# A decoder layer with attention replaced by an LRU, a Toeplitz mixer and routed experts: the norm of the next group, the query products and the Toeplitz tables are arranged anew

## The chip, the cores and the metric

One NeuronCore of a Trainium2 chip runs the whole kernel in one launch. The metric is device time in microseconds (us); the times given are medians over executions. The engines are PE (TensorE, matmuls), DVE (VectorE), ACT (ScalarE), POOL (GpSimd) and SP (SyncE, which here only issues DMAs).

## The reference, cut to what matters

`x` is 16 sequences of 128 tokens with 256 features. Everything is fp32.

```python
# block 1: gated linear recurrence and an MLP
xn = rmsnorm(x, norm1_w)
left  = gelu(xn @ left_W + left_b)
right = rg_lru(causal_depthwise_conv(xn @ right_W + right_b, conv_w, conv_b), ...)   # two gates, a scan over time
x1 = left * right @ out_W + out_b + x
x1n = rmsnorm(x1, norm2_w)
x = layernorm(x + gelu(x1n @ up1_W) * (x1n @ up2_W) @ down_W + down_b + x1)          # biases of up left out here
# block 2: 16 heads of width 8 over the 128 tokens; the features (256) are the time axis of the convolution
kv  = einsum('bhil,bhjl->bijhl', ctx, ctx)            # symmetric in i, j: 36 pairs per head
out = causal_conv(kv, ssm_kernel) + kv * D            # a 256-tap Toeplitz product per head
x = layernorm(x + einsum('bijhl,bhil->bjhl', out, x))
# block 3: 64 experts, top 6, capacity 64 over the first tokens that vote for an expert, and a shared expert
x = layernorm(x + moe(x))
```

## The kernel before, in words

The 16 sequences are worked in G = 4 groups of NB = 4 sequences (512 tokens). `over_groups` (L265) calls `step(gh, gt, gs)` on every engine: the head (block 1) of group gh, the tail (block 2, the norm and the router of block 3) of group gh-1, and the shared expert of group gh-2, in one step. There are five steps: step 0 has a head only, step 1 head and tail, steps 2 and 3 (the body of a hardware loop, L269) all three, and the last one tail and shared expert. Then come the voting rounds and shared expert of the last group, 32 pairs of routed experts, and the final sums and norm. Each engine has its own instruction stream, written out in order by hand; semaphores tie them together, and an engine that waits holds everything behind it.

**Start.** SP issues (L293 to L316) x of group 0, four constants, five weight matrices on one semaphore (`weights_in`), then `krep_dram`, a copy of the padded taps with 128 rows per head in DRAM, the context, the shared weights, and behind a wait the read of the Toeplitz tables `toep` from `krep_dram` with a stride one shorter than a row (L308). Then it zeroes the accumulation buffer `y_dram` (L314 to L316, 6.6 MB) and loads x and context of the further groups (L317). PE's first dense product waits for all five weights (L747). POOL adds D to the diagonal of the 16 tables (L385, L388) before it forms the residual sums `xo = x + out_b` (L407) and `xs = x + down_b` (L413), and the pair products of the context (L397).

**Head.** ACT squares and sums x (`mean_square`, L518), takes the root (L529); DVE scales x to `xn` (`norm_apply`, L1015); PE transposes it into `tb` (L671); DVE copies it to `xT` (`feature_copy`, L1020); PE forms right and left (`dense`, L677); ACT evacuates (L542, L546); DVE does the 4-tap convolution (L1095, L1101); PE forms two gates; ACT evacuates (L553) and takes tanh and exp (L559, L561) and root (L568); DVE multiplies (L1117 to L1130), scans (L1132) and multiplies by left (L1135, `lr_s`); PE forms the output product (L803); DVE adds (L1143); a second norm (L518, L578, L1146, L1015, L671, L1020); six times two up products (L829, recorded at L677), gelu on ACT (L588) and product on DVE (L1168); then four blocks of down products (L840), and residual and statistics on DVE (L1206, L1210).

**Tail.** PE multiplies the Toeplitz tables into the pair products (`conv`, L723 to L725, heads 0 to 7 at the start of the step, 8 to 11 behind the dense products, 12 to 15 behind the gates), ACT evacuates to `ycv` (L513). DVE normalises block 1's output to `x2` (L1072), PE transposes, DVE copies to `q` (L1107). `query_products` (L964) multiplies q into ycv and sums over i: for each distance d of the pair (i, j) two products into `tmp` (L975) and two sums into `acc` (L980), 29 instructions for a group of heads. DVE has 11 heads, in slices of five instructions between its L1168 (L1170), POOL has 5. PE transposes `acc` (L859), then norm, router product (L877), softmax, top 6 and votes on DVE.

**Shared.** `votes_by_expert` (L709) puts the votes of group gs by expert; DVE picks the first 64 tokens of each in 8 `rounds` of max and replace (L1037, L1039), four before its 4-tap convolution and four after the copy to q (L1087, L1109). The shared expert is L696 and L705 on PE, L506 on ACT, L1050 and L1055 on DVE.

**Waits.** In the loop a wait's value is computed in a register (`wait_apart`, L256). `keep_clock` (L680) issues matmuls of zeros where PE has nothing to do: 8 at the start, 7 in step 0 and 5 in step 1 behind the gates, 6 in the last step.

## Time and profile before

| | |
|---|---|
| median of 3 executions | 668.96 us |
| lowest, highest | 667.96, 676.25 us |
| profiled execution: time, span | 671.55 us, 669.9 us |
| mean granted TensorE clock, as a share of 2.4 GHz | 0.892 |
| busy: PE, DVE, POOL, ACT | 522.3, 373.4, 277.8, 212.7 us |
| down products end (step 0, 1, 2, 3) | 110.9, 202.8, 307.0, 411.2 us |
| experts begin | 499.6 us |

The rows below come from one profiled execution. A row gives the start in us, the time from the start to the end of the group, the engine, the line, what is written and read, and in brackets the idle time of the engine before it and what ended it. A matmul in fp32 leaves two records. A PE record of 512 columns takes 0.43 us at 2.4 GHz and 0.85 us at 1.2 GHz.

### The profile page before, as it was taken

To read this page: it belongs to the slowest core of one execution; us is meant where nothing else is said; L and a number is where in the kernel's file an instruction comes from. 1 tells how busy PE (TensorE), PEld (TensorE's weight loads), DVE (VectorE), ACT (ScalarE), POOL (GpSimd) and SP (SyncE) were. 2 spreads that over 40 slices of the span, in tenths; PEclk is the share of its full clock that TensorE was granted. 3 is DMA by queue.
4 is the path that set the end of the run, shared out by engine and by line. 5 is a ranking of instruction groups with operands and counts; after the bars stand their busy time and mean duration, and the time that the engine had idled before them with its cause. 6 is when DMAs were issued, how large, how long until landed. Compare 5 with 4: busy or idle time off the path is not lost.

```text
span 669.9 us, 7127 instructions
## 1 busy us (share of the span) xinstructions
PE 522.3 (78%) x2181; PEld 313.8 (47%) x2181; DVE 373.4 (56%) x850; ACT 212.7 (32%) x431; POOL 277.8 (41%) x340
## 2 busy tenths in 40 slices
PE   5863699975986987996887998948779887779075
PEld 2322349543466543566543468615345433334065
DVE  2357224553968983967985766995753212123037
ACT  4350232452124472315472314311203221213024
POOL 1029301537505437503545701690036455457500
PEclk9795699986998988999998999968979988889579
DMA  8996100100001101001200000886229999975596
GB/s 300 173 362 264 33 0 1 32 1 31 0 1 39 32 1 31 1 32 40 96 0 0 0 31 35 265 238 186 97 55 274 314 300 290 303 239 66 55 380 247
DMA packets 30702, 81.17 MB, mean 121 GB/s; under 512 B 3248, under 2 KB 16048, under 8 KB 30544
## 3 DMA queue, kind: packets, MB, share of 16 engines
q1 hardware_dynamic: 23328, 66.48, 30.9%
q0 software_dynamic: 7344, 14.32, 9.3%
q8 instruction: 15, 0.25, 0.1%
q14 instruction: 15, 0.12, 0.1%
HBM read 62.80 MB, written 21.13 MB: 125 GB/s over the span
## 4 chain that ended last, share of the span: by engine, by line
PE 49%; DVE 27%; issue 11%; DMA 5%; ACT 5%; SPq 1%; DVEq 0%; ACTq 0%; POOLq 0%
PE mb L677 15%; PE kb L840 6%; PE mb L920 5%; PE kb L939 4%; PE kb L705 4%; DMA y_dram<-cregion,y_all 3%; DVE first L1037 3%; DVE cand L1039 3%; PE kb L803 3%; DVE hregion L1015 2%; DVE cregion L980 2%; DMA wregion<-in_w_down_dram 2%; DVE cregion L975 2%; PE mb L960 2%; PE tb L960 1%
## 5 line engine op out<-in xcount | busy, mean ns | idle before, releaser
L677 PE MATMUL mb<-hregion,wregion 128*128 128x512 f32 x320 | 155.3, 645 | 16.6 <-DVE hregion L1020 5.4
L677 PEld LDWEIGHTS mb<-hregion,wregion 128*128 128x128 f32 x320 | 65.3, 208 | 99.5 <-issue 85.7
L397 POOL TENSOR_TENSOR cregion<-ctxT 128x256 f32<-128x256 f32 (+7 forms) x128 | 68.4, 568 | 77.9 <-PE mb L725 77.9
L463 POOL DMA_INDIRECT y_dram<-cregion,y_all x32 | 50.3, 1573 | 44.3 <-DVE cregion L1309 40.2
L1309 DVE TENSOR_SCALAR cregion<-kb,prob 128x256 f32<-128x256 f32 x32 | 15.5, 484 | 77.5 <-issue 67.2
L840 PE MATMUL kb<-wregion,hregion 128*128 128x256 f32 x192 | 43.7, 382 | 5.2 <-DVE hregion L1168 5.2
L588 ACT ACTIVATE hregion<-mb,cols 128x512 f32<-128x512 f32 x24 | 16.5, 687 | 92.5 <-PE mb L677 92.5
L454 POOL DMA_INDIRECT hregion<-rows_dram,idx_all x32 | 31.3, 978 | 32.1 <-DVE idx_all L1283 19.0
L1168 DVE SCALAR_TENSOR_TENSOR hregion<-mb,cols,hregion 128x512 f32<-128x512 f32 x24 | 17.9, 746 | 43.9 <-PE mb L677 43.9
L840 PEld LDWEIGHTS kb<-wregion,hregion 128*128 128x128 f32 x192 | 35.7, 190 | 13.0 <-DVE hregion L1168 4.6
L980 POOL TENSOR_TENSOR cregion<-cregion 128x280 f32<-128x280 f32 (+6 forms) x56 | 40.6, 725 | 2.2
L975 POOL TENSOR_TENSOR cregion<-cregion 128x280 f32<-128x280 f32 (+6 forms) x56 | 37.7, 673 | 4.4
L437 POOL DMA_DIRECT2D rows_dram<-rows x4 | 3.1, 770 | 82.6 <-DVE rows L1244 82.6
L696 PE MATMUL mb<-x3T,wsh 128*128 128x512 f32 x64 | 30.3, 626 | 5.0 <-ACT cregion L513 4.0
L683 PE MATMUL mb<-zeros,ident 128*128 128x512 f32 x52 | 28.7, 712 | 6.0 <-ACT cregion L513 2.9
L975 DVE TENSOR_TENSOR cregion<-cregion 128x616 f32<-128x616 f32 (+6 forms) x56 | 31.6, 565 | 1.6
L980 DVE TENSOR_TENSOR cregion<-cregion 128x616 f32<-128x616 f32 (+6 forms) x56 | 31.7, 567 | 0.7
L803 PE MATMUL kb<-wregion,hregion 128*128 128x256 f32 x64 | 17.7, 438 | 18.4 <-DVE hregion L1135 18.4
L671 PE MATMUL tb<-ident,hregion 128*128 128x128 f32 x64 | 12.0, 350 | 22.9 <-DVE hregion L1015 22.9
L513 ACT ACTIVATE cregion<-mb 128x288 f32<-128x288 f32 x64 | 23.8, 408 | 17.3 <-PE mb L725 17.3
L705 PE MATMUL kb<-wshd,shh 128*128 128x256 f32 (+1 forms) x96 | 26.8, 442 | 3.2 <-DVE shh L1050 3.2
L615 ACT ACTIVATE wregion<-mb 88x256 f32<-88x256 f32 x32 | 12.2, 380 | 51.9 <-PE mb L929 51.9
(186 smaller groups left out, 1000.3 us busy)
## 6 DMA issues: line engine op xcount, KB each, us to landing
hregion<-in_w_experts_dram SPq DMA_DIRECT2D x12, 704.0 KB
wregion<-in_w_experts_dram SPq DMA_DIRECT2D x11, 704.0 KB
y_dram<-zeros SPq DMA_DIRECT2D x4, 1536.0 KB, 14.4
hregion<-in_w_experts_down_dram SPq DMA_DIRECT2D x12, 352.0 KB
cregion<-in_w_experts_dram SPq DMA_DIRECT2D x6, 704.0 KB
wregion<-y_dram SPq DMA_DIRECT2D x8, 512.0 KB, 6.6
hregion<-y_dram SPq DMA_DIRECT2D x8, 512.0 KB, 14.0
wregion<-in_w_experts_down_dram SPq DMA_DIRECT2D x11, 352.0 KB
```

Of the source, the lines that this page charges most:

```text
L397: last = e.tensor_tensor(v.kv[:, hb % 2, :, :, DOFF[d] * NB:DOFF[d] * NB + n], cx[:, :, :, 0:n], cx[:, :, :, d * NB:d * NB + n], ALU.mult)
L454: e.indirect_dma_start(out=v.xg[:, r, :], out_offset=None, in_=v.rows_dram[:, :], in_offset=bass.IndirectOffsetOnAxis(ap=v.idx_all[:, p:p ...
L463: e.indirect_dma_start(out=v.y_dram[:, :], out_offset=bass.IndirectOffsetOnAxis(ap=v.y_all[:, p:p + 1], axis=0), in_=v.dout[:, r, :], in_o ...
L677: last = e.matmul(bank, w[:, c, n0:n0 + P], rhs[:, c, :], start=(c == 0), stop=(c == C - 1))
L683: e.matmul(bank[:], v.ident[:], v.zeros[:, 0:512], start=True, stop=True)
L696: last = e.matmul(banks[k][0:n, :], v.wsh[:, c, k * FS + f * P:k * FS + f * P + n], v.x3T[:, c, :], start=(c == 0), stop=(c == C - 1))
L705: last = e.matmul(kb[k][:, b * D:(b + 1) * D], v.shh[0:n, f, t0:t0 + S], v.wshd[0:n, f, :], start=(f == 0), stop=(f == NF - 1))
L803: last = e.matmul(kb[k][:, b * D:(b + 1) * D], v.left[:, c, t0:t0 + S], v.wo[:, c, :], start=(c == 0), stop=(c == C - 1))
L840: last = e.matmul(kb[k][:, b * D:(b + 1) * D], v.mlp[:, j, t0:t0 + S], v.wdn[:, j, :], start=(j == 0), stop=(j == FJ - 1))
L920: last = e.matmul(mb[p % 2][x * CAP:(x + 1) * CAP, 0:2 * FE], v.xgT[:, p % 2, c, x * CAP:(x + 1) * CAP], wgu[:, x, c, :], start=(c == 0), ...
L975: steps.did(e.tensor_tensor(v.tmp[:, t, :, heads, 0:n], v.q[:, :, heads, cols], y, ALU.mult))
L980: steps.did(e.tensor_tensor(v.acc[:, :, heads, cols], v.acc[:, :, heads, cols], v.tmp[:, t, :, heads, 0:n], ALU.add))
```

## The change: what it does

The taps are loaded to 16 partitions, DVE adds D to tap 0, and they are written back to DRAM once. Each partition p then reads 256 taps of each head from offset p on (a Hankel table, 2 MB in rows of 1 KB), and PE multiplies by a flipped identity (8 matmuls of 512 columns, behind the gates of step 0, where `keep_clock` was), which turns it into the Toeplitz table; ACT evacuates it (8 copies). Each weight has a semaphore of its own. The norm of group g+1 is made in step g: squares and root on ACT after the gelus, scaling on DVE after the query products, transposes on PE (into `mb`) behind the first down product and the transposes of acc, the copy to xT on DVE before the first residual. The votes and all 8 rounds of group gs now stand behind the copy to q. POOL makes the products of the context first, the residual sums behind q, and waits for x1n before it adds `xo` to `xs`. The query products go by 32 pairs of feature half and head: distances d and 8-d share one full-width temporary, so that 15 instructions do what 29 did; DVE has 22 of the 32 and POOL 10, the same shares. The loops over groups are written out. `load_x(1)` stands ahead of the zeroing of `y_dram`, `load_ctx(1)` behind it.

```diff
@@ -30,7 +30,8 @@
 HEADS = S // HD
-HEADS_DVE = 11
+CH = 2 * HEADS
+CH_DVE = 22
...
@@ -185,13 +187,14 @@
         v.ctxT = sb("ctxT", [P, C, S * NB])
-        cregion = sb("cregion", [P, 10752])
+        cregion = sb("cregion", [P, 11008])
...
         v.ycv = take(C * HEADS * PW, cregion).rearrange("p (c h n) -> p c h n", c=C, h=HEADS)
+        v.hankel = v.ycv.rearrange("p c h n -> p (c h n)")[:, 0:HEADS * 2 * P].rearrange("p (h n) -> p h n", h=HEADS)
...
         v.acc = take(C * HEADS * HD * NB, cregion).rearrange("p (c h n) -> p c h n", c=C, h=HEADS)
-        v.tmp = take(2 * C * HEADS * (HD - 1) * NB, cregion).rearrange("p (t c h n) -> p t c h n", t=2, c=C, h=HEADS)
+        v.tmp = take(2 * CH * HD * NB, cregion).rearrange("p (t g n) -> p t g n", t=2, g=CH)
...
@@ -266,7 +270,7 @@
     step(1, 0, None)
-    with e.Fori(2, G) as g:
+    for g in range(2, G):
...
@@ -290,23 +294,28 @@
+        e.dma_start(v.taps, v.kpad_in).then_inc(s["taps_in"], 16)
+        e.dma_start(v.d_sb[:], v.d_in.rearrange("o h -> h o")).then_inc(s["taps_in"], 16)
         load_x(0)
...
+        e.dma_start(v.cols[:], v.cols_in).then_inc(s["consts_in"], 16)
+        e.dma_start(v.wlr, v.wlr_in).then_inc(s["w_lr"], 16)
+        e.dma_start(v.outb[:], v.outb_in.to_broadcast((P, D))).then_inc(s["consts_in"], 16)
+        e.dma_start(v.downb[:], v.downb_in.to_broadcast((P, D))).then_inc(s["consts_in"], 16)
+        e.dma_start(v.wg, v.wg_in).then_inc(s["w_gates"], 16)
+        e.dma_start(v.wo, v.wo_in).then_inc(s["w_out"], 16)
         load_ctx(0)
+        e.dma_start(v.wup, v.wup_in).then_inc(s["w_up"], 16)
+
+        e.wait_ge(s["taps_s"], 1)
+        e.dma_start(v.taps_dram, v.taps).then_inc(s["taps_out"], 16)
+        e.dma_start(v.wdn, v.wdn_in).then_inc(s["w_down"], 16)
+        e.wait_ge(s["taps_out"], 16)
+        k = v.taps_dram[0:HEADS, 0:1]
+        e.dma_start(v.hankel, bass.AP(k.tensor, k.offset, [[1, P], [KW, HEADS], [1, 2 * P]])).then_inc(s["tables"], 16)
...
+        load_x(1)
...
@@ -314,7 +323,8 @@
         e.dma_start(yv[:, NBLK, rest:], v.zeros[:, 0:D]).then_inc(s["zero_out"], 16)
-        with e.Fori(1, G) as g:
+        load_ctx(1)
+        for g in range(2, G):
...
@@ -373,19 +384,17 @@
+        e.memset(v.flip, 0.0).then_inc(s["flip_s"], 1)
+        e.wait_ge(s["flip_s"], 1)
+        e.affine_select(out=v.flip, in_=v.flip, compare_op=ALU.not_equal, fill=1.0, base=1 - P,
+                        pattern=[[E, 2], [1, E]], channel_multiplier=1).then_inc(s["flip_s"], 1)
...
+        e.wait_ge(s["consts_in"], 16 * 3)
...
@@ -399,34 +408,32 @@
         def step(gh, gt, gs):
+            if gt is not None:
+                products(gt, 2)
+                products(gt, 3)
...
-
-                if not (isinstance(gh, int) and gh == 0):
+                if gt is not None:
+
+                    wait(e, s["q_s"], 2 * gt + 2)
...
                 if gt is not None:
-                    products(gt, 2)
-                if gt is not None:
...
                     .then_inc(s["xs_s"], 1)
-            elif gt is not None:
-                products(gt, 2)
-            if gt is not None:
-                products(gt, 3)
-            if gh is not None:
...
                 wait(e, s["x1_s"], 2 * gh + 2)
+                wait(e, s["x1n_s"], 4 * gh + 4)
...
                 wait(e, s["q_s"], 2 * gt + 2)
-                for f in query_products(e, v, psteps, slice(HEADS_DVE, HEADS)):
+                for f in query_products(e, v, psteps, slice(CH_DVE, CH)):
...
@@ -505,6 +512,12 @@
+        def taps_turned(n0, banks):
+            for n, bank in enumerate(banks):
+                e.wait_ge(s["turned"], n0 + n + 1)
+                e.activation(v.toep[:, 2 * (n0 + n):2 * (n0 + n) + 2, :], bank[:].rearrange("p (h n) -> p h n", h=2), ACT.Copy)\
+                    .then_inc(s["toep_s"], 1)
...
@@ -518,17 +531,18 @@
-            if head:
-                wait(e, s["x_in"], 16 * gh + 16)
-                if not (isinstance(gh, int) and gh == 0):
-                    wait(e, s["x1_tr"], 2 * gh)
+            def norm_root(g):
+                wait(e, s["x_in"], 16 * g + 16)
+
+                wait(e, s["x1_tr"], 2 * g)
                 mean_square(v.xin, v.ss1, "ss1_s")
-                wait(e, s["ss1_s"], gh + 1)
-                if not tail:
-                    e.wait_ge(s["consts_s"], 1)
+                wait(e, s["ss1_s"], g + 1)
+                e.wait_ge(s["consts_s"], 1)
                 e.activation(v.rms1, v.ss1, ACT.Sqrt, scale=1.0 / D, bias=v.eps_rms[:]).then_inc(s["rms1_s"], 1)
-                if not tail:
-                    softplus()
+
+            if head and not tail:
+                norm_root(0)
+                softplus()
...
@@ -566,6 +580,9 @@
                     e.activation(v.th[:, c, :], v.th[:, c, :], ACT.Sqrt).then_inc(s["mult_s"], 1)
+            if not tail:
+                taps_turned(0, (kb[0], kb[1], v.tb[0], v.tb[1]))
+                taps_turned(4, mb)
...
@@ -587,6 +604,8 @@
                         .then_inc(s["gelu_s"], 1)
+                if gh + 1 < G:
+                    norm_root(gh + 1)
...
@@ -711,6 +730,10 @@
+        def turn_taps(n0, banks):
+            for n, bank in enumerate(banks):
+                e.matmul(bank[:], v.flip, v.hankel[:, 2 * (n0 + n):2 * (n0 + n) + 2, :], start=True, stop=True).then_inc(s["turned"], 1)
...
@@ -725,39 +748,44 @@
-            if tail:
-                e.wait_ge(s["d_done"], 2)
+            def features(g):
+                wait(e, s["xn_s"], 4 * g + 4)
+                for k in range(2):
+                    transposes(v.xn, k, "x_tr", mb)
+
+            if tail:
+                e.wait_ge(s["toep_s"], HEADS // 2)
+                if head:
+                    wait(e, s["xT_s"], 4 * gh + 4)
...
             if head:
-                wait(e, s["xn_s"], 4 * gh + 4)
-                if gs is not None:
-                    wait(e, s["x3T_s"], 2 * gt)
-                    wait(e, s["logit_read"], gt)
-                for k in range(2):
-                    transposes(v.xn, k, "x_tr")
-            if gs is not None:
-                wait_apart(e, v, s["y_s"], 2 * gt + 2)
-                wait_apart(e, v, s["dve_r"], RDVE * gt)
-                votes_by_expert(gs)
-            if head:
-                e.wait_ge(s["weights_in"], 16 * 5)
+                if not tail:
+                    features(0)
+                e.wait_ge(s["w_lr"], 16)
...
                     dense(mb[k][:], v.wlr, (k + 2) % 4 * P, v.xT, "lr_done")
+            if gs is not None and not head:
+                wait_apart(e, v, s["y_s"], 2 * gt + 2)
+                wait_apart(e, v, s["dve_r"], RDVE * gt)
+                votes_by_expert(gs)
...
                 wait(e, s["x2_s"], 4 * gt + 4)
-                if not head:
-                    wait(e, s["x3T_s"], 2 * gt)
-                    wait(e, s["logit_read"], gt)
+                wait(e, s["x3T_s"], 2 * gt)
+                wait(e, s["logit_read"], gt)
...
                     transposes(v.x2, k, "x2_tr")
+                if gs is not None and head:
+                    wait(e, s["y_s"], 2 * gt + 2)
+                    wait(e, s["dve_r"], RDVE * gt)
+                    votes_by_expert(gs)
...
@@ -787,11 +816,17 @@
                         wait(e, s["conv_evac"], HEADS * gt + HEADS)
+                        keep_clock(mb[3], 5)
                     else:
+                        e.wait_ge(s["flip_s"], 2)
+                        e.wait_ge(s["tables"], 16)
+                        turn_taps(0, (kb[0], kb[1], tb[0], tb[1]))
                         wait(e, s["gate_s"], 4 * gh + 4)
-                    keep_clock(mb[3], 5 if tail else 7)
+                        turn_taps(4, mb)
+                        e.wait_ge(s["toep_s"], 2)
                 wait(e, s["lr_s"], C * gh + C)
+                e.wait_ge(s["w_out"], 16)
...
@@ -823,7 +860,7 @@
                         elif i < 4:
-                            wait(e, s["gate_s"], 4 * gh + i + 1)
+                            wait(e, s["toep_s"], HEADS // 4 + i + 1)
...
@@ -861,6 +899,8 @@
             if head:
+                if gh + 1 < G:
+                    features(gh + 1)
...
@@ -961,29 +1001,46 @@
+def query_products(e, v, steps, part):
+
+    n_part = part.stop - part.start
+    WIDE = HD * NB
+    y = v.ycv.rearrange("p c h n -> p (c h) n")[:, part]
+    q = v.q.rearrange("p c h n -> p (c h) n")[:, part]
+    acc = v.acc.rearrange("p c h n -> p (c h) n")[:, part]
+    tmp = v.tmp[:, :, part]
+
+    def pair_of(ap, at, step, n):
+        return bass.AP(ap.tensor, ap.offset + at, [list(ap.ap[0]), [step, 2], list(ap.ap[-2]), [1, n]])
+
+    def both(d, low):
...
         n = (HD - d) * NB
...
+        lo = tmp[:, low]
+        hop = (CH * WIDE) * (1 - 2 * low)
+        yd = y[:, :, DOFF[d] * NB:DOFF[d] * NB + n]
+        wait(e, steps.sem, steps.base + steps.n)
+        steps.did(e.tensor_tensor(pair_of(lo, d * NB, hop - d * NB, n), pair_of(q, 0, d * NB, n), pair_of(yd, 0, 0, n), ALU.mult))
+
+    def diagonal():
+        steps.did(e.tensor_tensor(acc, q, y[:, :, 0:WIDE], ALU.mult))
+
+    def middle():
+        d = HD // 2
+        n = d * NB
+        yd = y[:, :, DOFF[d] * NB:DOFF[d] * NB + n]
+        wait(e, steps.sem, steps.base + steps.n)
+        steps.did(e.tensor_tensor(pair_of(tmp[:, 0], n, -n, n), pair_of(q, 0, n, n), pair_of(yd, 0, 0, n), ALU.mult))
+
+    def add(t, behind):
+        wait(e, steps.sem, steps.base + steps.n - behind)
+        steps.did(e.tensor_tensor(acc, acc, tmp[:, t], ALU.add))
+
+    parts = [diagonal]
+    for d in range(1, HD // 2):
+        parts += [lambda d=d: both(d, 1), lambda d=d: both(HD - d, 0), lambda: add(0, 0), lambda: add(1, 0)]
+    parts += [middle, lambda: add(0, 0)]
+    assert len(parts) == QSTEPS
...
@@ -1009,16 +1066,18 @@
         e.wait_ge(s["tnum_s"], 1)
+        e.wait_ge(s["taps_in"], 32)
+        e.tensor_tensor(v.taps[:, P - 1:P], v.taps[:, P - 1:P], v.d_sb[:], ALU.add).then_inc(s["taps_s"], 1)
...
-        def feature_copy(k, name, done):
+        def feature_copy(k, name, done, banks=tb):
...
                 e.tensor_scalar(v.xT[:, c, k * 2 * S:(k + 1) * 2 * S].rearrange("p (b s) -> p b s", b=2),
-                                tb[k][:].rearrange("p (b c s) -> p b c s", b=2, c=C)[:, :, c, :],
+                                banks[k][:].rearrange("p (b c s) -> p b c s", b=2, c=C)[:, :, c, :],
...
@@ -1057,12 +1116,21 @@
             head, tail = gh is not None, gt is not None
+            def norm_one(g):
+                wait(e, s["rms1_s"], g + 1)
+                e.reciprocal(v.inv1, v.rms1).then_inc(s["inv1_s"], 1)
+                wait(e, s["inv1_s"], g + 1)
+                norm_apply(v.xn, v.xin, v.inv1, "xn_s")
+
+            def features(g):
+                for k in range(2):
+                    wait(e, s["x_tr"], 2 * g + k + 1)
+                    feature_copy(k, "norm1", "xT_s", mb)
...
                 hsteps.begin(gh)
-                wait(e, s["rms1_s"], gh + 1)
-                e.reciprocal(v.inv1, v.rms1).then_inc(s["inv1_s"], 1)
-                wait(e, s["inv1_s"], gh + 1)
-                norm_apply(v.xn, v.xin, v.inv1, "xn_s")
+                if not tail:
+                    norm_one(0)
...
@@ -1073,18 +1141,15 @@
                 if not tail:
-                    e.wait_ge(s["consts_in"], 16 * 4)
-                for k in range(2):
-                    wait(e, s["x_tr"], 2 * gh + k + 1)
-                    feature_copy(k, "norm1", "xT_s")
-                if not tail:
+                    e.wait_ge(s["consts_in"], 16 * 3)
+                    features(0)
...
                     e.tensor_scalar(v.lru[:, 0], v.lru[:, 0], LRU_C, None, ALU.mult).then_inc(s["lru_s"], 1)
-            if gs is not None:
+            if gs is not None and not head:
...
@@ -1107,6 +1172,9 @@
             if gs is not None:
+                if head:
+                    votes_in(gs)
+                    rounds(0, 4)
...
@@ -1167,15 +1235,17 @@
                                            in1=v.gl[:, j % 2, :], op0=ALU.add, op1=ALU.mult).then_inc(s["h_s"], 1)
-                    for f in parts[5 * j:5 * j + 5]:
+                    for f in parts[QPART * j:QPART * j + QPART]:
...
                 for n, f in enumerate(parts):
-                    if gs is not None and n in (4, 8, 12):
-                        shared_rows(gs, n // 4 - 1)
-                    if gs is not None and n == 24:
+                    if gs is not None and n in (2, 4, 6):
+                        shared_rows(gs, n // 2 - 1)
+                    if gs is not None and n == 12:
...
                     f()
+            if head and gh + 1 < G:
+                norm_one(gh + 1)
...
@@ -1211,6 +1281,8 @@
             if head:
+                if gh + 1 < G:
+                    features(gh + 1)
```

## Rows read from the trace of the kernel before

**Rows 1.** The page: busy time by engine, its share of the span, instructions.

```profile
PE 522.3 (78%) x2181; PEld 313.8 (47%) x2181; DVE 373.4 (56%) x850; ACT 212.7 (32%) x431; POOL 277.8 (41%) x340
```

**Rows 2.** Timeline of step 0, all engines, 8 to 69 us.

```profile
8.14 1.14 DVE L1015 TENSOR_SCALAR hregion<-hregion,st 128x256 f32<-128x256 f32 x4
...
17.69 9.96 PE L677 MATMUL mb<-hregion,wregion 128*128 128x512 f32 x16 [5.37 <-DMA wregion<-in_w_down_dram]
...
45.07 0.68 DVE L1130 TENSOR_TENSOR hregion<-hregion 128x512 f32<-128x512 f32 x1
...
45.84 4.57 POOL L385 TENSOR_TENSOR cregion<-ident,d_sb 128x2048 f32<-128x2048 f32 x1 [42.46 <-DMA wregion<-krep_dram]
...
47.04 3.91 DVE L1135 TENSOR_TENSOR hregion<-hregion 128x512 f32<-128x512 f32 x1
...
61.87 6.62 PE L803 MATMUL kb<-wregion,hregion 128*128 128x256 f32 x16 [16.44 <-DVE hregion L1135]
```

**Rows 3.** Timeline of DVE in step 1: the same instruction, and the last of the sequence, 144 to 150 us.

```profile
144.59 0.69 DVE L1130 TENSOR_TENSOR hregion<-hregion 128x512 f32<-128x512 f32 x1 [0.17 <-ACT hregion L568]
...
149.16 0.69 DVE L1135 TENSOR_TENSOR hregion<-hregion 128x512 f32<-128x512 f32 x1
```

**Rows 4.** DMA issues, from the page of DMAs: KB each, us to landing.

```profile
krep_dram<-in_kpad_dram SPq DMA_DIRECT2D x1, 3064.0 KB, 29.8
...
wregion<-krep_dram SPq DMA_DIRECT2D x1, 2048.0 KB, 9.8
```

**Rows 5.** Timeline of PE: the dense products that open the head of steps 1, 2 and 3; behind the gates of step 3.

```profile
119.04 7.11 PE L677 MATMUL mb<-hregion,wregion 128*128 128x512 f32 x16 [1.36 <-issue]
...
216.88 7.65 PE L677 MATMUL mb<-hregion,wregion 128*128 128x512 f32 x16 [0.33 <-DVE hregion L1020]
...
320.48 7.13 PE L677 MATMUL mb<-hregion,wregion 128*128 128x512 f32 x16 [0.35 <-DVE hregion L1020]
...
353.16 3.72 PE L803 MATMUL kb<-wregion,hregion 128*128 128x256 f32 x16 [1.01 <-DVE hregion L1135]
```

**Rows 6.** Timeline of DVE in step 3, and a round of the last step.

```profile
341.91 1.23 DVE L1117 TENSOR_TENSOR hregion<-hregion 128x1024 f32<-128x1024 f32 x1
...
359.92 2.94 DVE L1015 TENSOR_SCALAR hregion<-hregion,st 128x256 f32<-128x256 f32 x4
...
420.60 0.75 DVE L1037 MAX8 first<-cand 64x8 f32<-64x576 f32 x1
...
422.23 0.75 DVE L1037 MAX8 first<-cand 64x8 f32<-64x576 f32 x1
```

**Rows 7.** Groups by shape: query products, and a copy of a PSUM bank on ACT.

```profile
L975 DVE TENSOR_TENSOR cregion<-cregion 128x616 f32<-128x616 f32 x8 | 7.9, 984 | 0.3
...
L598 ACT ACTIVATE x3T<-tb 128x512 f32<-128x512 f32 x8 | 4.3, 594 | 10.5 <-PE tb L671 10.5
...
L975 DVE TENSOR_TENSOR cregion<-cregion 128x264 f32<-128x264 f32 x8 | 3.5, 433 | 0.3
...
L975 DVE TENSOR_TENSOR cregion<-cregion 128x88 f32<-128x88 f32 x8 | 2.0, 246 | 0.2
```

**Rows 8.** Timeline of POOL in step 1: query products with DVE idle.

```profile
157.81 1.63 POOL L975 TENSOR_TENSOR cregion<-cregion 128x280 f32<-128x280 f32 x2
...
164.11 1.29 POOL L975 TENSOR_TENSOR cregion<-cregion 128x200 f32<-128x200 f32 x2
```

**Rows 9.** Timeline of PE and DVE: down products of step 1, and the last step.

```profile
187.59 2.86 PE L840 MATMUL kb<-wregion,hregion 128*128 128x256 f32 x12 [2.04 <-DVE hregion L1168]
...
461.20 1.29 DVE L1186 TENSOR_TENSOR u<-tb,x 128x512 f32<-128x512 f32 x2 [2.43 <-DMA y_dram<-u]
```

**Rows 10.** Windows: us, PE, PEld, DVE, ACT, POOL busy, granted clock, DMA share, GB/s.

```profile
7.00:12.00 5.00, 5.00 (x18) 2.56 (x17) 1.33 (x6) 4.14 (x8) 0.00 (x0) 1.00 1.02 410
...
18.00:24.00 6.00, 6.00 (x8) 2.38 (x8) 0.55 (x1) 0.69 (x1) 0.00 (x0) 0.55 1.08 177
...
62.00:70.00 8.00, 6.49 (x16) 4.90 (x16) 1.38 (x2) 0.74 (x4) 7.15 (x17) 0.64 0.00 1
```

63 lines of the change are left out of this document (17 added, 46 removed).

## The prediction

> **What bounds the kernel now.** I read the page first, then the chain that ended last, then the timeline of each engine by step, and the groups by shape for prices. PE is busy for 78% of the span, DVE for 56% [rows 1], and in the chain PE has half the time and DVE a quarter. So PE is the resource, and time is to be had only where PE waits. These places differ by step. In step 0 PE waits 5.37 us for the last of five weights although it needs the first, and 16.44 us for DVE's scan and product [rows 2]. That second wait is not DVE work: L1135 takes 3.91 us there [rows 2] and 0.69 us in step 1 [rows 3], because POOL's table sums (4.57 us, and one more of that size behind) run at the same time. At the head of steps 1, 2 and 3 PE stands still for the norm of x (dense products at 119.04, 216.88 and 320.48, while the step before ended at 110.9, 202.8 and 307.0) [rows 5]. The reader should see in each row's bracket who was late.
>
> **Start, step 0.** x's DMA goes out two issues later, about 1 us. The dense product now needs its own weights alone, so up to 5.4 us are free [rows 2]. But POOL's two residual sums (L407 and L413, 1024 elements each; POOL takes 2.1 ns an element and 0.25 us, so 2.4 us [rows 8]) no longer stand behind the tables; they become ready when the constants land, at about 9 us, just when DVE scales x (4 instructions, 1.14 us alone, 8.14) [rows 2]. In step 3, DVE's same four instructions took 2.94 us beside one such POOL sum [rows 6]. Beside two they would take up to 5 us, end near 15 instead of 9.3, and the dense product would start at 17.4 instead of 17.69: gain 0.3. If DVE is first, it starts at 13.9, and PE, with a pause of 1.5 instead of 5.4 us, may keep 2.4 GHz (7 to 12 us) instead of falling to 1.2 GHz (clock 0.55, 18 to 24 us) [rows 10], which is worth some 3 us more: gain 6.8. I take 1.5, near the lower end, since POOL's start and DVE's are within a microsecond of each other.
>
> **The tables.** The DRAM copy of 3064 KB (29.8 us to landing) goes, and the read stays as large (2048 KB, 9.8 us) [rows 4]. It is issued when the 24 KB of taps have landed behind some 4 MB of earlier loads; at 300 GB/s (an estimate from the 410 and 177 GB/s of the windows [rows 10]) this is at 16 us, and the table lands at 26 to 29, ahead of the end of the gates at 37. POOL's two sums leave DVE's way. From L1130 to the output product step 1 takes 144.59 to 149.9, 5.3 us [rows 3]; step 0 took 45.07 to 61.87, 16.8 us [rows 2]. Gain 11.5. The new work is 8 matmuls, 16 records of 0.43 us, 6.9 us in the place of `keep_clock`, and 8 ACT copies of 0.594 us [rows 7], 4.8 us behind ACT's roots. Both lie beside the 5.3 us of DVE; PE needs only two of the copies before its output product, the other six before the up products 7 us on. I cost them at nothing. Without this cover they would cost up to 5 us. Moving `load_x(1)` ahead of the zeroing costs nothing: x of group 1 is wanted after the gelus, 20 us later. The zeroing (6.6 MB, 15 us of issue) and `load_ctx(1)` behind it have until step 1. Separate semaphores for the later weights wait for nothing: all have landed by 20 us.
>
> **The norm made ahead.** The transposes (8 records, 1.0 us of PE) move from the head of steps 1 to 3 into steps 0 to 2: plus 1.1 us in each of these (3.3 in all), and minus their share at the head. ACT's squares, table and root take 3.6 us behind the last gelu, then DVE 1.3; PE in this time has its first down block (2.9 us [rows 9]) and, with a tail, the transposes of acc, so xn is late by at most 0.3 us. DVE's copies (1.7 us) stand before a residual that has 2.7 us of idle time behind it. With x ready, the dense products start when the 8 heads of convolution end, 5.95 us into the step (24 triples at 0.245). Before, they started 8.1, 14.0 and 13.5 us in [rows 5]. Gross gain 2.2, 8.1 and 7.5.
>
> **The rounds behind q.** In steps 2 and 3 this is partly given back, because DVE fills the gap with nothing. Step 3 counted from the dense products: right lands at 2.4 and 4.2 us, the 4-tap convolution ends at 8.7, copy to q at 10.7, votes at 11.5, eight rounds at 24.6 (pitch 1.64 us, 420.60 to 422.23 [rows 6]), so L1117 starts at 24.9. (An estimate: landing times, the convolution's 4.5 us, q's 2.0 and the rounds are taken as step 3 shows them.) Before, it started at 341.91 - 320.48 = 21.4 [rows 5, 6]. The gates then are no longer last, DVE is. Behind L1117 the way to the output product is 7.9 to 8.9 us, and before it waited a little for ACT's exp, so 1.3 (step 2) to 2.0 us (step 3) are given back at the output product. The net gain there is 6.8 and 5.5.
>
> **POOL behind x1n.** DVE's second scaling no longer meets the sum L424: 2.94 us become 1.14 [rows 6, 2], in steps 1, 2 and 3: 1.8 each. POOL's queue: the products of group gt come first, and PE wants the first at 12 us into the step; the query products start 2.3 us later, and have over 20 us until PE transposes acc.
>
> **Query products.** Elements stay the same (22 x 480 = 10560 on DVE). An instruction of 88 elements takes 246 ns and one of 264 takes 433 [rows 7], so 1.06 ns an element and 0.15 us each; with POOL at work 616 take 984 [rows 7], 1.4 ns an element. 14 instructions fewer are 2.1 us less on DVE in each of four passes. Only what DVE is late for counts: in step 1 the down products wait 2.04 us for L1168 [rows 9], I take 1.8; in steps 2 and 3 shared work covers it, 0; in the last step DVE is the chain, but the shared expert's product and the storing DMA stand between (2.43 us of its wait [rows 9]): I take 3.0 in all.
>
> **Clock.** PE's pause before the output product of steps 2 and 3 grows from 1.0 [rows 5] to about 4 us. After a long pause the same 16 records took 6.62 us [rows 2] at clock 0.64 [rows 10], against 3.72 [rows 5]. Cost 0 to 2.9 twice, I take 1.0 each.
>
> **The sum.** Step 0: 1.5 + 11.5 - 1.1 = 11.9. Step 1: 2.2 + 1.8 + 1.8 - 1.1 = 4.7. Step 2: 6.8 + 1.8 - 1.1 = 7.5. Step 3: 5.5 + 1.8 = 7.3. Last 3.0. Clock -2.0. Together 32.4. The experts and final sums (from 499.6 us on) keep their length. The profiled execution took 671.55 us, 2.6 over the median, so 639.2 for it and 668.96 - 32.4 = 636.6 for the median; I say 636.5.
>
> **Weighed against the Trainium skill.** A rule that speaks against wide instructions is in "SBUF — State Buffer", section "Who interferes with whom": DVE with two SBUF inputs and POOL lock each other out for a whole instruction. Step 0 agrees (3.91 us for 0.69 [rows 2, 3]). By it, fewer and longer POOL instructions hold DVE longer each time; as a mechanism of this kernel it is the second rival. "Runtime: NRT & Kernel Launch", section "Instruction fetch mechanics", says that a taken branch can force a fetch of code; the trace shows no gap on PE at the loop's turn (the last product ends at 307.0, and the table products follow at once), so by the trace unrolling gives nothing, and by the page it would give one fetch, which no row here prices.
>
> **Rivals.** *First: x is scaled before POOL's sums, and the clock stays up.* Start gain 6.8 instead of 1.5, clock loss 0: 636.5 - 7.3 = 629. For it: DVE's scaling begins at about 9.2 and takes 1.1. Against: the constants land at the same time. 0.2. *Second: the port.* The POOL query products (up to 560 elements, about 1.4 us) and DVE's run one after the other in all four passes: DVE's 13.4 us (10560 x 1.06 ns and 15 x 0.15 us [rows 7]) wait for 5 to 6 of POOL's 13.8 (4800 x 2.1 ns and 15 x 0.25 us [rows 8]), beyond the slack of 2 us: 4 x 3.5 = 14, so 650. For it: 984 ns where 803 are due [rows 7]. Against: POOL starts 9 us before DVE and has few left. 0.12. *Third: the table is late.* A hot 24 KB in DRAM, read 85 times over, at half the speed (20 us): it lands at 37 to 40, where PE wants it at 37; the turning then ends up to 3 us behind the scan and ACT's copies delay x1; with a low clock 8 us: 644. 0.13. *Fourth, the other side: the paired products are slow.* Their access patterns step over two halves with runs of 4 to 28 elements; were they to cost more per element on DVE, 4928 elements in each of four passes would be late. The gain of 32.4 is gone when each pass is 8.1 + 3 of slack late, 2.3 ns an element more (three times today's price); at 3.0 ns more it is 4 x (14.8 - 3) = 47 late, 684, slower by over 2%. Against: today's form has as many dimensions and runs of 4 to 28 too, at 246 ns for 88 elements [rows 7]. 0.03.
>
> **How the numbers follow.** Forecast 0.52. The range takes in the first rival and the start's full gain (down to 624), and the second and third (up to 650). Two per cent, 13.4 us, is about what a measurement of this kernel can tell from no change. Faster than 655.6: all but part of the rivals' upper ends, 0.94; within 2% 0.04; slower 0.02.
>
> **What would show it.** Right: the output product of step 0 at about 49 us with no long DVE instruction before; dense products 6 us after each step's first convolution, with no idle time; L1117 ending the gates' wait in steps 2 and 3; the second scaling at 1.1 us. Wrong: a PE wait on the DMA of the Hankel table; PE waiting for xn behind the first down block; query products beyond 1.5 us on DVE; a clock of 0.55 through the up products.

## The result, and the profile after

The changed kernel took 649.07 us (median of 4 executions, 646.63 to 655.09). Beside it the kernel before took 672.55 us, and the ratio is 0.967 (95% interval 0.956 to 0.977): faster by 3.3% where 4.8% were forecast. 649.07 lies at the upper edge of the range, 624 to 650. A second series gave a ratio of 0.960 (0.950 to 0.970). All ratios leave out executions over 1.5% above the fastest of the same kernel, and of the traces shown only e1's is of such a slower execution.

To see where the time went I cut each trace where DVE ends the last residual sum of a step (L1206 before, L1276 after), and at PE's first expert product. The two traces of the changed kernel agree within 0.1 us on each of these marks.

| us | step 0 | step 1 | step 2 | step 3 | last step | experts begin | rest of the span |
|---|---|---|---|---|---|---|---|
| before | 111.7 | 91.9 | 104.1 | 104.2 | 87.7 | 499.6 | 170.3 |
| changed | 93.9 | 91.5 | 99.7 | 98.4 | 86.9 | 470.4 | 173.8 |
| changed, second trace | 93.9 | 91.5 | 99.7 | 98.4 | 86.9 | 470.5 | 170.7 |
| gain | 17.8 | 0.4 | 4.4 | 5.8 | 0.8 | 29.2 | |
| forecast | 11.9 | 4.7 | 6.5 | 6.3 | 3.0 | 32.4 | 0 |

(The forecast's 2.0 us for the clock are taken off steps 2 and 3 here.) The sum up to the experts is nearly right, and the steps are not: step 0 gave 6 us more, the others gave 9 us less. So the near hit is in part luck. Step 0 also varies from trace to trace: in the ten traces of kernels that differ in nothing that step 0 executes it took 91.3 to 96.2 us. Busy time on the page answers to [rows 1]; PE has as much work as before in less time:

```profile
PE 520.1 (81%) x2183; PEld 316.0 (49%) x2183; DVE 368.1 (57%) x795; ACT 217.0 (34%) x439; POOL 251.9 (39%) x284
```

**Step 0** answers to [rows 2]. Timeline of the changed kernel, DVE, POOL and PE:

```profile
8.75 1.14 DVE L1074 TENSOR_SCALAR hregion<-hregion,st 128x256 f32<-128x256 f32 x4
...
10.48 2.34 POOL L420 TENSOR_TENSOR hregion<-hregion,outb 128x1024 f32<-128x1024 f32 x1 [6.70 <-DMA downb<-in_down_b_dram]
...
14.27 7.11 PE L696 MATMUL mb<-hregion,wregion 128*128 128x512 f32 x16 [1.48 <-DVE hregion L1079]
24.88 8.61 PE L696 MATMUL mb<-hregion,wregion 128*128 128x512 f32 x16 [3.51 <-DVE hregion L1166]
...
40.19 0.68 DVE L1198 TENSOR_TENSOR hregion<-hregion 128x512 f32<-128x512 f32 x1
...
44.75 0.69 DVE L1203 TENSOR_TENSOR hregion<-hregion 128x512 f32<-128x512 f32 x1
...
45.54 5.09 PE L838 MATMUL kb<-wregion,hregion 128*128 128x256 f32 x16 [5.18 <-ACT wregion L518]
```

The reader sees DVE scale x before POOL's sums begin, the dense products at 14.27 at full clock (16 records in 7.11 us), and the scan with no stretched instruction: L1203 takes 0.69 us where L1135 took 3.91. From the first product behind the roots to the output product are 5.35 us, as forecast. (The last bracket names an ACT copy. By the code PE wants only the first two of the eight, which had ended by 41.9; the last it waits for is L1203, which ends at 45.44.)

**Step 1.** Timeline of PE in the changed kernel:

```profile
98.86 7.03 PE L696 MATMUL mb<-hregion,wregion 128*128 128x512 f32 x16
...
129.65 3.72 PE L838 MATMUL kb<-wregion,hregion 128*128 128x256 f32 x16 [0.98 <-DVE hregion L1203]
...
166.88 4.54 PE L877 MATMUL kb<-wregion,hregion 128*128 128x256 f32 x12 [3.78 <-DVE hregion L1236]
```

The dense products start without a wait 5.8 us after the down products of step 0, where they took 8.1 before. DVE's first slice of the MLP is 4.7 us earlier in the step (at 52.2, before 56.9). Then it is lost: from the first to the last h DVE takes 20.0 us where it took 18.3, the first down block waits 3.78 us for the last h (2.04 before [rows 9]), and it takes 4.54 us instead of 2.86, most of it at half the clock.

**Step 3.** Timeline of the changed kernel, DVE at the head, then PE behind the gates:

```profile
289.31 2.76 DVE L1324 TENSOR_TENSOR votes<-mask,tnum 128x256 f32<-128x256 f32 x1
292.10 0.73 DVE L1327 TENSOR_SCALAR tnum<-tnum 128x4 f32<-128x4 f32 x1
...
292.94 3.61 DVE L1140 TENSOR_SCALAR x<-hregion,mv,st 128x256 f32<-128x256 f32 x4
...
317.06 1.23 DVE L1185 TENSOR_TENSOR hregion<-hregion 128x1024 f32<-128x1024 f32 x1
```

```profile
326.18 6.42 PE L838 MATMUL kb<-wregion,hregion 128*128 128x256 f32 x16 [3.79 <-DVE hregion L1203]
...
339.27 14.00 PE L696 MATMUL mb<-hregion,wregion 128*128 128x512 f32 x32 [1.31 <-DVE hregion L1079]
...
367.54 2.86 PE L877 MATMUL kb<-wregion,hregion 128*128 128x256 f32 x12 [1.99 <-DVE hregion L1236]
```

L1324 takes 2.76 us where the same product took 0.43 at 312.01 before, and the four x2 scalings 3.61 for 1.46: POOL's products of the table, moved to the head, run at 289.2 to 296.3. DVE's gate product comes 27.0 us after the first dense product instead of the forecast 24.9; PE then pauses 3.8 us, and its output product takes 6.42 us instead of 3.72 [rows 5]. Two things stand against this. DVE's head was not free of POOL before either: beside a POOL sum and eight products L1255 took 2.23 us, where the same instruction takes 0.17 in e1, and the scaling of x took 2.27 for 1.14. And PE gets clock back further on. Its first 32 records of up products take 14.00 us, and took 17.02 before (15.69 in step 2):

```profile
365.46 17.02 PE L677 MATMUL mb<-hregion,wregion 128*128 128x512 f32 x32 [1.39 <-DVE hregion L1020]
```

So my theory for the experiments was: from step 1 on DVE is last, not PE; it loses time beside POOL, PE's pauses grow, and PE's clock falls behind them. Rivals: the query products' new form is itself slower or saves nothing; the norm made ahead was never the limit; the last part of the kernel got longer by the change.

### The profile page after: what moved, and what is told of

Read it like the earlier page. It is cut to its first block, busy times and chain, and to the rows that moved or that the text cites. A ratio compares the mean times of both kernels' runs of the same rounds, so it can differ in the third digit from the quotient of the medians.

```text
span 644.2 us, 6592 instructions
## 1 busy us (share of the span) xinstructions
PE 520.1 (81%) x2183; PEld 316.0 (49%) x2183; DVE 368.1 (57%) x795; ACT 217.0 (34%) x439; POOL 251.9 (39%) x284
## 4 chain that ended last, share of the span: by engine, by line
PE 50%; DVE 31%; issue 10%; DMA 4%; ACT 3%; POOL 0%; POOLq 0%; DVEq 0%; SPq 0%
PE mb L696 14%; PE kb L877 7%; PE mb L960 5%; PE kb L979 4%; DVE cand L1098 4%; DMA y_dram<-cregion,y_all 4%; DVE first L1096 4%; PE kb L838 3%; PE mb L702 2%; PE kb L724 2%; DVE cregion L1037 2%; DVE hregion L1166 2%; DVE x L1140 2%; PE kb L715 2%; PE mb L1000 2%
## 5 line engine op out<-in xcount | busy, mean ns | idle before, releaser
L696 PE MATMUL mb<-hregion,wregion 128*128 128x512 f32 x320 | 145.8, 613 | 9.9 <-DVE hregion L1079 6.0
L696 PEld LDWEIGHTS mb<-hregion,wregion 128*128 128x128 f32 x320 | 62.0, 197 | 85.8 <-issue 73.3
L406 POOL TENSOR_TENSOR cregion<-ctxT 128x256 f32<-128x256 f32 (+7 forms) x128 | 63.1, 527 | 40.2 <-PE mb L748 40.2
L877 PE MATMUL kb<-wregion,hregion 128*128 128x256 f32 x192 | 45.5, 393 | 8.7 <-DVE hregion L1236 8.7
L431 POOL TENSOR_TENSOR hregion<-hregion 128x1024 f32<-128x1024 f32 x4 | 9.4, 2346 | 85.3 <-issue 85.3
L1236 DVE SCALAR_TENSOR_TENSOR hregion<-mb,cols,hregion 128x512 f32<-128x512 f32 x24 | 17.9, 745 | 35.2 <-PE mb L696 35.2
L838 PE MATMUL kb<-wregion,hregion 128*128 128x256 f32 x64 | 22.0, 518 | 15.4 <-DVE hregion L1203 10.3
L1037 POOL TENSOR_TENSOR cregion<-cregion 128x320 f32<-128x320 f32 x28 | 31.8, 1135 | 2.2
L1037 DVE TENSOR_TENSOR cregion<-cregion 128x704 f32<-128x704 f32 x28 | 31.2, 1113 | 0.7
L634 ACT ACTIVATE wregion<-mb 88x256 f32<-88x256 f32 x32 | 12.2, 380 | 54.1 <-PE mb L969 45.4
L1023 POOL TENSOR_TENSOR cregion<-cregion 128x560 f32<-128x560 f32 (+5 forms) x24 | 29.7, 1236 | 1.9
L1374 DVE TENSOR_TENSOR wregion<-mb,wregion 128x176 f32<-128x176 f32 x32 | 10.8, 337 | 32.5 <-ACT wregion L648 29.4
L1023 DVE TENSOR_TENSOR cregion<-cregion 128x1232 f32<-128x1232 f32 (+5 forms) x24 | 28.9, 1205 | 0.6
## 6 DMA issues: line engine op xcount, KB each, us to landing
hregion<-y_dram SPq DMA_DIRECT2D x8, 512.0 KB, 12.9
```

The lines of the kernel that those rows point to most:

```text
L406: last = e.tensor_tensor(v.kv[:, hb % 2, :, :, DOFF[d] * NB:DOFF[d] * NB + n], cx[:, :, :, 0:n], cx[:, :, :, d * NB:d * NB + n], ALU.mult)
L696: last = e.matmul(bank, w[:, c, n0:n0 + P], rhs[:, c, :], start=(c == 0), stop=(c == C - 1))
L838: last = e.matmul(kb[k][:, b * D:(b + 1) * D], v.left[:, c, t0:t0 + S], v.wo[:, c, :], start=(c == 0), stop=(c == C - 1))
L877: last = e.matmul(kb[k][:, b * D:(b + 1) * D], v.mlp[:, j, t0:t0 + S], v.wdn[:, j, :], start=(j == 0), stop=(j == FJ - 1))
L1023: steps.did(e.tensor_tensor(pair_of(lo, d * NB, hop - d * NB, n), pair_of(q, 0, d * NB, n), pair_of(yd, 0, 0, n), ALU.mult))
L1037: steps.did(e.tensor_tensor(acc, acc, tmp[:, t], ALU.add))
```

## The experiments

All steps by the marks of the table above; ratios are to the kernel before on the same chip.

**e1: POOL behind x2,** in POOL's `step`.

> The changed kernel, but POOL waits for x2 before the table products of the group being finished (one wait, nothing else). Port theory (DVE's scaling and votes are stretched because POOL's products moved beside them): the votes product falls from 2.76 us to under 1.3, the four x2 scalings from 3.6 us to under 2.0, in every step head from step 2 on; the first gate-side product of DVE then starts at most 25 us after the first dense product in step 3 (27.0 before), and steps 2 and 3 are each 1.5 to 3 us shorter: in all 3 to 6 us below the changed kernel. Rival (the contention only moves: POOL's products then stretch the 4-tap convolution and the copy to q by as much): the same DVE time between the end of the step before and the gates, no change within 1 us. A second rival: PE waits for the later tables at head 8, and the step grows.

```diff
             if gt is not None:
+                wait(e, s["x2_s"], 4 * gt + 4)
                 products(gt, 2)
```

Ratio 0.953 (0.943 to 0.963); steps 1 to 3: 93.2, 98.5, 97.9; last step 84.0. Timeline of DVE in e1, step 3:

```profile
291.04 0.43 DVE L1325 TENSOR_TENSOR votes<-mask,tnum 128x256 f32<-128x256 f32 x1
...
291.79 1.38 DVE L1141 TENSOR_SCALAR x<-hregion,mv,st 128x256 f32<-128x256 f32 x4
294.47 0.76 DVE L1161 TENSOR_SCALAR hregion<-hregion,cols 128x512 f32<-128x512 f32 x1 [1.30 <-ACT hregion L557]
...
296.65 5.41 DVE L1167 SCALAR_TENSOR_TENSOR hregion<-hregion,cols 128x512 f32<-128x512 f32 x6
```

The stretching is gone, 5.1 us of it, so its cause is shown. But the gate product is only 1.1 us earlier in the step: DVE now waits 2.3 us for ACT's copies of the dense products, and the 4-tap convolution takes 5.41 us beside POOL instead of 4.06. In step 3 the first down block also took 4.54 us instead of 2.86, so 1.7 us of what the wait gave there went with the clock. Both theory and rival were half right. Only the last step, where DVE has no convolution, kept most of it (2.9 us); e8, e9 and e14, which have the same wait, took 83.4 to 84.5 us there.

**e2 and e15: the last parts behind the last h.** The same kernel twice, on two chips.

> The changed kernel with the 15 parts of DVE's query products cut 3, 3, 3, 2, 2, 2 over the six slices of the MLP instead of 3, 3, 3, 3, 3, 0. Theory (in step 1 the first down block waits 3.78 us and runs at the lower clock because all parts stand ahead of the last h): that wait falls to under 1.8 us in step 1, and the first down block takes 2.9 instead of 4.5 us; step 1 is 2.5 to 4 us shorter; steps 2 and 3, where shared work covers it, gain 0 to 1.5. Rival (the time is only moved to the transposes of acc, which want the last part): the step keeps its length within 0.7 us.

```diff
+QCUT = (0, 3, 6, 9, 11, 13, 15)
...
-                    for f in parts[QPART * j:QPART * j + QPART]:
+                    for f in parts[QCUT[j]:QCUT[j + 1]]:
```

> The kernel with the cut alone once more. Its steps repeat: 88.0, 97.3 and 94.8 us for steps 1 to 3. If its last part, 179.7 us in its first trace, belongs to the kernel, it is 178 to 182 again; if it belongs to the run or the chip, it comes out with that of the other kernels, 170 to 176.

e2: ratio 0.951 (0.943 to 0.959), steps 91.3, 88.0, 97.3, 94.8. e15: ratio 0.949 (0.945 to 0.954), steps 96.2, 89.9, 97.4, 96.3. So where the parts are cut is worth 1.6 to 3.6 us in each of steps 1 to 3, and the transposes of acc don't give it back. The steps did not repeat as I had expected of e15: step 1 is 1.9 and step 3 is 1.5 us longer than in e2. In step 1 the down block starts after 1.78 (e2) or 1.06 us (e15) and takes 2.86. The two traces differ in what no edit made: 4.9 us in step 0 and 1.9 in step 1. Windows of 7.2 us, from 28.5 us into step 1, e2 and then e15 (columns as in [rows 10]):

```profile
119.80:127.00 7.20, 6.26 (x10) 2.41 (x10) 6.85 (x10) 2.56 (x5) 4.00 (x5) 0.76 0.01 2
```

```profile
124.70:131.90 7.20, 4.56 (x10) 1.82 (x10) 6.86 (x10) 2.56 (x5) 4.00 (x5) 1.00 0.01 2
```

PE had done the same ahead of this. In e2 the clock falls under the five filler products (6.26 us) and is back for the output product (3.72). In e15 the fillers run at full clock in 4.56 us, the pause behind them is 2.7 instead of 1.0 us, and the output product takes 5.41. In step 0, likewise, the 16 gate records behind a pause of 3.2 to 3.5 us took 7.13 us in e2, 8.61 in the changed kernel and 10.19 in e15. The last part took 176.1 us in e15 and 179.7 in e2, so at least 3.6 us of its spread are not the kernel's.

**e3: fillers ahead of the output product of steps 2 and 3.**

> The changed kernel with four filler products (ident by zeros, 3.4 us of PE) ahead of the wait for the scan in steps 2 and 3, into the bank that the output product overwrites. Clock theory (after PE's pause of 3.8 us the output product runs at 1.2 GHz, 6.4 us for 16 records, and the transposes and part of the up products behind it too): the output product takes 3.7 us in steps 2 and 3, and each of these steps is 2.5 to 3.5 us shorter; in all 5 to 7 us. Rival (DVE is last anyway: its x1 sum and the norm only start earlier by part of it): 1 us a step or less. Steps 0 and 1 unchanged.

```diff
+                if gs is not None:
+                    wait(e, s["voteT_s"], gs + 1)
+                    keep_clock(kb[1], 4)
                 wait(e, s["lr_s"], C * gh + C)
```

Ratio 0.964 (0.958 to 0.970); steps 2 and 3: 96.7 and 97.4. The output product takes 3.72 us in both. Step 2 gained 3.0 us, step 3 only 1.0, since there the first down block then took 4.54 us instead of 2.86: the clock fell at a later pause.

```profile
323.35 3.72 PE L841 MATMUL kb<-wregion,hregion 128*128 128x256 f32 x16 [0.35 <-DVE hregion L1206]
...
361.99 4.54 PE L880 MATMUL kb<-wregion,hregion 128*128 128x256 f32 x12 [1.99 <-DVE hregion L1239]
```

**e4: four rounds into DVE's waits.**

> The changed kernel with the last four of the eight rounds of MAX8 and MATCH_REPLACE8 of steps 2 and 3 moved from ahead of DVE's gate product to its waits behind the scan (behind the shared rows, between and behind the two x1 sums, behind the second scaling). Theory (DVE's rounds are last before the gates' product and make PE pause): the gate product starts 5.5 to 6.6 us earlier, or where the gates end (about 21.4 us after the first dense product, as before the change); PE's pause before the output product goes to 1 us or less and its 16 records take 3.7 us; what the moved rounds then cost behind it is 1.6 us at most for those ahead of the second scaling. Steps 2 and 3 shorter by 4 to 7 us each, 8 to 14 us in all. Rival (the rounds are late for what follows as they were for what stood ahead): gain under 2 us a step.

```diff
-                rounds(4, 8)
-                keep_first()
...
                 shared_rows(gs, 1)
+                rounds(4, 5)
...
+                    if gs is not None and k == 0:
+                        rounds(5, 6)
+                if gs is not None:
+                    rounds(6, 7)
...
                 norm_apply(v.xn, v.xo, v.inv2, "x1n_s")
+                if gs is not None:
+                    rounds(7, 8)
+                    keep_first()
```

Ratio 0.967 (0.961 to 0.973); steps 2 and 3: 98.9 and 96.2. The gate product came 6.7 us earlier in the step (25.3 for 32.0), and the step gained 0.8 and 2.2. PE in e4, step 3:

```profile
321.56 3.72 PE L838 MATMUL kb<-wregion,hregion 128*128 128x256 f32 x16 [1.62 <-DVE hregion L1204]
326.98 3.67 PE L715 MATMUL kb<-x3T,wsh 128*96 128x512 f32 x8 [1.70 <-DVE hregion L1213]
...
334.53 2.11 PE L696 MATMUL mb<-hregion,wregion 128*128 128x512 f32 x3 [2.99 <-DVE hregion L1079]
```

The rival nearly won: rounds ahead of an x1 sum and of the feature copies are late for these (waits of 1.70 and 2.99 us). The clock took another part: the first 32 records of up products took 15.70 us in both steps for 14.00 in the changed kernel, and in step 2 the first down block took 4.29 for 2.86. DVE's only wait long enough, 5.6 us, is behind the copies.

**e5: the norm at the head again.** `norm_root`, `norm_one` and `features` at the head of each step, as before the change.

> The changed kernel with the norm of x made where it was before the change: root, scaling, transposes (into tb, with the waits of before) and feature copies at the head of each step, votes and four rounds ahead of the 4-tap convolution; tables, weights, POOL's order and the query products stay changed. By the sum of the forecast (norm ahead gives 6.8 and 5.5 us net in steps 2 and 3, 2.2 in step 1, and costs 1.1 in steps 0 to 2): step 0 1.1 us shorter than in the changed kernel, step 1 1.1 longer, step 2 5.7 longer, step 3 5.5 longer, 11 in all. Rival (DVE is last in these steps, so what is made ahead was not the limit, and the rounds behind q cost as much as the norm gave): steps 2 and 3 each longer by less than 3 us.

Ratio 0.978 (0.972 to 0.985); steps 92.8, 94.6, 103.6, 101.8. The norm made ahead costs 1.1 us in step 0, to the digit (the first down block ends at 84.3 here and at 84.4 in the changed kernel), and gives 3.1, 3.9 and 3.4 in steps 1 to 3. The forecast's own net, with features and clock off, was 1.1, 4.7 and 4.5. The rival (under 3 us) fails.

**e6: the query products of before.** The 29 instructions of the old `query_products`, five behind each h.

> The changed kernel with the query products of before (29 instructions over 11 of 16 heads, five behind each h, four behind the last). Forecast's term: step 1 1.8 us longer, last step 3 us longer, steps 2 and 3 the same. Theory now (the wide products save DVE nothing, because beside POOL's long ones each waits for one of them, and all of them stand ahead of the last h): step 1 is 0 to 2.7 us shorter, its first down block takes 2.9 us again and waits about 2 instead of 3.8, the last step is longer by 1 us or less. Rival (the new form is worth what the instruction counts say): the six slices of the MLP in steps 2 and 3 take DVE 2 us more than 24.4.

Ratio 0.979 (0.972 to 0.986); steps 94.4, 92.0, 102.8, 101.6, last 90.3. Here my theory fell: the new form is worth 0.5 us in step 1, but 3.1 and 3.2 in steps 2 and 3, where the forecast had 0, and 3.4 in the last step (forecast 3.0). Groups of DVE over the six slices of step 3, first the kernel before, then e6:

```profile
L975 DVE TENSOR_TENSOR cregion<-cregion 128x616 f32<-128x616 f32 (+6 forms) x13 | 7.3, 561 | 0.3
L980 DVE TENSOR_TENSOR cregion<-cregion 128x616 f32<-128x616 f32 (+5 forms) x12 | 7.0, 587 | 0.2
```

```profile
L1017 DVE TENSOR_TENSOR cregion<-cregion 128x616 f32<-128x616 f32 (+6 forms) x14 | 9.1, 653 | 0.4
L1022 DVE TENSOR_TENSOR cregion<-cregion 128x616 f32<-128x616 f32 (+6 forms) x14 | 8.8, 630 | 0.2
```

The same instructions cost a mean of 642 ns in place of 573 (and the three that the first stretch lacks are the smallest). POOL's own query products point to the reason, step 3 before and changed:

```profile
360.07 0.92 POOL L972 TENSOR_TENSOR cregion<-cregion 128x320 f32<-128x320 f32 x1
```

```profile
339.23 0.86 POOL L1026 TENSOR_TENSOR cregion<-cregion 128x320 f32<-128x320 f32 x1
```

DVE's first part came at 372.96 before and comes at 343.79 now. POOL's lead has shrunk from 12.9 to 4.6 us: 3.4 of this because its queue now waits for x1n ahead of the last residual sum, the rest because DVE itself gets from the x1 sums to its first slice sooner (10.5 us in place of 15.4, 3.0 of it by the clock of the up products). More of the two engines' products run side by side, and DVE's instructions take longer there. That fewer instructions pay less often fits the numbers; no run shows it apart.

**e7: x scaled behind POOL's sums.**

> The changed kernel, but the first scaling of x (step 0) waits for the end of POOL's two residual sums. Theory (step 0 gained 4.8 us ahead of the gates where 1.5 were forecast, because DVE scaled x before POOL's sums began and PE's pause stayed short): the first dense product starts at 17 to 18.5 us instead of 14.3, and the gates' product of DVE 3 to 5 us later, at 37 to 39; step 0 is 3 to 5 us longer, and so is the kernel up to the experts; steps 1 to 3 keep their lengths. Rival (the start gain comes from the weights having their own counts, and 3 us of delay are covered by PE's full clock): step 0 longer by less than 2 us.

```diff
                 wait(e, s["rms1_s"], g + 1)
+                if not tail and g == 0:
+                    wait(e, s["xs_s"], 1)
```

Ratio 0.977 (0.971 to 0.982); step 0 101.8, the others unchanged. The first dense product starts at 20.76 us, 6.5 later, and step 0 is 7.9 longer, more than I expected: behind a pause of 6.81 us PE's dense products took 9.66 us in place of 7.11. The order of two engines at 8.75 and 10.48 us decides some 8 us.

**e8: three mends together.** The cut of e2, the wait of e1, and the rounds one behind each x1 sum and two behind the feature copies.

> The changed kernel with three mends: DVE's query parts cut 3, 3, 3, 2, 2, 2; POOL's later table products behind x2; and the last four rounds of steps 2 and 3 one behind each x1 sum and two behind the feature copies of x1, where DVE waited 3.9 to 5.6 us for the first up products. Theory: step 1 3 to 4 us shorter (as with the cut alone), steps 2 and 3 each 4 to 7 us shorter than in the changed kernel (2.4 to 3.6 from the cut, 2 to 4 from the rounds, 1 from POOL), last step 1 to 3 shorter; the experts start at 452 to 458 us instead of 470; the kernel takes 628 to 638 us. Rival (DVE with PE beside it is full over the MLP's slices, so what is gained ahead of them is lost in them): steps 2 and 3 no shorter than with the cut alone, 97.3 and 94.8 us.

Ratio 0.928 (0.921 to 0.935), 626.4 us. Steps 95.9, 89.9, 91.6, 90.7, last 84.2, experts from 452.3. Steps 2 and 3 shrank by 8.1 and 7.7 us. The mends alone gave 1.2, 2.4 and 0.8 us in step 2, 4.4 in sum (the rounds placed worse than here). With all three the gate product comes 24.1 us into steps 2 and 3, and PE's output product follows the shared experts with no idle time and takes 3.62 us.

**e9: the mends placed otherwise.** POOL's wait from step 2 on only, and three fillers ahead of step 0's output product.

> The kernel with three mends, but POOL waits for x2 in steps 2, 3 and the last only (in step 1 the wait made PE pause 2.7 us and run its output product at 5.4 us), and with three filler products in step 0 between the turned tables and the output product. Theory: step 1 falls from 89.9 to 88.0 us; in step 0 the output product takes 3.7 instead of 5.1 to 5.9 us, step 0 is 1 to 2 us shorter; steps 2 and 3 stay at 91.6 and 90.7; the experts start at 448 to 451 us, the kernel takes 622 to 627. Rival (the filler in step 0 delays the output product by as much as the clock gives): step 0 unchanged within 0.7.

Ratio 0.931 (0.922 to 0.941); steps 93.5, 90.0, 91.6, 90.4. Step 0's output product took 3.72 us, but the slices of the MLP started only 0.4 us earlier than in the changed kernel. Step 1 stayed at 90.0 with no wait of POOL in it, so that explanation of mine was wrong: it again had the short fillers (4.56 us) and an output product of 5.41 us, as in e8 and e15.

**e10: the same without POOL's wait.** The cut and the moved rounds.

> The kernel with the cut and the moved rounds, but POOL's products not behind x2. It tells how much of the 8 us by which steps 2 and 3 shrank is POOL's place. Theory (DVE's votes and x2 are stretched by about 5 us beside POOL's products, and with the rounds moved DVE is still last ahead of the gate product): the gate product of steps 2 and 3 starts 1 to 3 us later than the 24.1 us into the step of the three mends, and each step is 1 to 3 us longer, 92.5 to 94.5. Rival (additive as when it was alone): 1.1 us a step.

Ratio 0.940 (0.931 to 0.950); steps 94.1, 88.0, 92.3, 91.3, last 87.7. The gate product is 1.1 us later than in e8, and steps 2 and 3 are 0.7 and 0.6 longer: the rival, POOL's place is worth about as little here as alone, but for 3.5 us in the last step.

**e11: the changed kernel again,** the third line of the table above. Its last part, 170.7 us, lay below the expected 172 to 184.

> The changed kernel itself, once more, beside the others on one chip: how far its steps and its last part (from the first expert product on, 173.8 us) vary from run to run. Expected: steps within 0.5 us of 93.9, 91.5, 99.7, 98.4; the last part anywhere from 172 to 184 us, since it is bound by the loads of the experts' weights. If the last part always took 174, the difference of 4 us to the kernel before would be due to the change.

**e12: the kernel before with its loops written out.**

> The kernel before with its two loops written out and nothing else changed. Forecast said that this gives nothing. Expected: ratio to the kernel before within 0.995 to 1.005, steps 2 and 3 at 104.1 and 104.2 us, and the last part, from the first expert product on, longer than the 170.3 us of the one trace there is (174 to 182), if that one was a lucky one. Rival (a fetch of code at each turn of the loop): step 3 shorter by 1 to 3 us.

Ratio 1.008 (1.003 to 1.013); steps 110.8, 91.9, 103.9, 102.7, experts from 499.1, rest 172.8. Written-out loops give nothing, as forecast, and the ratio lies on the slow side of the expected 0.995 to 1.005. Step 3 is 1.5 us shorter, as the rival asked, but not by a fetch: its dense products start later in the step (14.2 us, before 12.8), and the 32 records of up products that took 17.02 us at 365.46 take 14.00. So it is the clock.

**e13: POOL's order of before.**

> The changed kernel with POOL's order of before: the residual sum for xo first, then the table products of head 8 to 11, the sum for xs, the products of head 12 to 15, and the last sum of a step beside DVE's second scaling. By the forecast's term (the second scaling takes 2.94 instead of 1.14 us, nothing else): steps 1, 2 and 3 each 1.8 us longer than 91.5, 99.7 and 98.4. By what the traces showed since (votes and x2 stretched by some 5 us beside the products that moved): steps 2 and 3 between 1 us shorter and 1 us longer, since both orders put POOL beside some work of DVE at the head; step 1 longer by 1 to 2.

The sum for xo stands ahead of `products(gt, 2)`, that for xs between the two:

```diff
-            if gt is not None:
-                products(gt, 2)
-                products(gt, 3)
...
-                    wait(e, s["q_s"], 2 * gt + 2)
...
+                    products(gt, 2)
                     wait(e, s["x2_s"], 4 * gh)
...
+            if gt is not None:
+                products(gt, 3)
...
                 wait(e, s["x1_s"], 2 * gh + 2)
-                wait(e, s["x1n_s"], 4 * gh + 4)
```

Ratio 0.968 (0.962 to 0.973); steps 96.1, 91.5, 103.6, 103.7. So the new order is worth 3.9 and 5.3 us in steps 2 and 3, not 1.8, and nothing in step 1; my expectation for it was wrong. DVE in e13, step 3:

```profile
295.01 4.98 DVE L1322 TENSOR_SCALAR mask<-pr 128x256 f32<-128x256 f32 x1
```

This instruction takes 0.33 us in the changed kernel. POOL's sum and eight products run from 295.26 to 301.4 without a gap, and DVE's instruction ends only after 5 us. A second sum and eight products then stretch the convolution (5.66 us for 4.06). On the other side the 15 query products of DVE take 15.2 us in this step, and 17.3 in the changed kernel.

**e14: all mends.** As e8, with three fillers in step 0 and seven instead of five in step 1.

> All mends: the cut 3, 3, 3, 2, 2, 2; POOL's later products behind x2; four rounds behind the x1 sums and copies; three filler products ahead of step 0's output product; and seven instead of five in step 1. Theory (in step 1 five fillers at full clock leave PE a pause of 2.7 us, and the output product then takes 5.4 us): step 1 takes 88.0 to 88.5 us instead of 89.9, its output product 3.7; step 0 93.5, steps 2 and 3 91.6 and 90.5; the experts start at 447 to 449 us. Rival (the clock falls elsewhere in step 1 instead): 90 us.

Ratio 0.934 (0.929 to 0.938), 630.05 us; steps 93.2, 88.0, 91.3, 90.7, last 83.4, experts from 446.6. The seven fillers took 6.28 us at full clock. In step 1 the output product kept the clock too, and in step 3 it follows with no pause:

```profile
121.70 6.28 PE L704 MATMUL mb<-zeros,ident 128*128 128x512 f32 x14 [2.90 <-ACT cregion L528]
128.94 3.72 PE L841 MATMUL kb<-wregion,hregion 128*128 128x256 f32 x16 [0.96 <-DVE hregion L1207]
```

```profile
309.23 3.62 PE L841 MATMUL kb<-wregion,hregion 128*128 128x256 f32 x16
```

The clock still falls elsewhere, at the start of step 1's up products and in step 3's shared expert (16 records in 8.83 us for 7.13). The kernel has the shortest way to the experts, 24 us shorter than the changed kernel, but by whole times it can't be told from e8 (the intervals overlap). Both beat the changed kernel by about 3%.

**The last part.** Windows of 80 us from the first expert product, of the kernel before, the changed one and e3:

```profile
499.60:579.60 80.00, 67.30 (x418) 33.27 (x418) 19.16 (x81) 20.86 (x64) 43.92 (x38) 0.89 0.98 289
```

```profile
470.40:550.40 80.00, 66.25 (x409) 32.41 (x410) 19.48 (x81) 20.81 (x63) 43.32 (x38) 0.89 0.98 281
```

```profile
467.10:547.10 80.00, 62.81 (x391) 30.82 (x390) 17.30 (x73) 19.94 (x60) 40.36 (x35) 0.89 0.96 263
```

The DMA engines are full in all three, and move 289, 281 and 263 GB/s; the rest of the span is 170.3, 173.8 and 183.7 us. I take it from this that the part is bound by the experts' weights; its length goes with the rate that they come at in all seventeen traces. Over these it was 170.3 to 183.7 us, with 173.8 and 170.7 for the changed kernel, 170.3 for that of before and 172.8 for its unrolled form. An effect of the change on it of a few us is not shown and not excluded.

## Why the prediction was wrong, and where it was right

**The step that failed** is the one on the query products, with the wait put in front of POOL's. The prediction had "2.1 us less on DVE in each of four passes" and put the wait for x1n at nothing, since POOL's queue "has over 20 us". What the traces show is DVE's busy time in its query products (the rows `cregion<-cregion`), in us:

| | step 1 | step 2 | step 3 | last step |
|---|---|---|---|---|
| before: old form, POOL's old order | 15.7 | 15.9 | 15.6 | 17.9 |
| changed: 15 wide instructions, POOL behind x1n | 16.7 | 17.3 | 17.3 | 16.4 |
| e6, the old form in the new order | 17.7 | 18.6 | 18.6 | 18.3 |
| e13, the new form in POOL's old order | 14.6 | 15.2 | 15.2 | 15.7 |

DVE's time rose by 1.0 to 1.7 us in three of the four passes. The form does save (1.0 to 1.9 us in the new order), but POOL's new order costs 2.1 us a step in steps 1 to 3. Step 1 shows what this does to the sum: it was 4.7 us ahead at its first h, with 4.0 forecast for the norm and the scaling; then, where 1.8 us more were to come, the slices lost 1.8, the clock of the first down block 1.7 and the features about 1, and 0.4 was left. The last step gave 0.8 of 3.0: the form gave 3.4 there (e6), and POOL's products beside DVE's votes and x2, which the prediction put at nothing, took 2.9 (e1).

**The whole.** The forecast took 32.4 us off. The traces have 29.2 up to the experts (step 0 5.9 over its forecast; step 1 4.3, step 2 2.1, step 3 0.5 and the last step 2.2 under theirs), 3.5 given back in the last part, which was to keep its length, and 0.8 outside the span: 24.9 between the two profiled executions, 7.5 short. The other 5.1 of the 12.6 us miss come from comparing medians: the 668.96 that I subtracted from is 2.6 us below its profiled execution, and the 649.07 is 2.4 above its own. Later series put the kernel before at 673 to 675 us.

**Start (1.5 forecast).** The first rival's order came true, DVE ahead of POOL's sums. DVE's gate product came 4.9 us earlier (39.1 to 34.3), not 6.8. The dense products kept the clock (7.11 us for 9.96); but DVE's convolution took 5.37 us beside POOL's products, 4.06 before, and behind a pause of 3.5 us the gates took 8.61 us, nearly the 8.83 of before, not the 7.13 that they take at full clock. I chose the lower of two ends 6.5 us apart because POOL's start was near, and this was wrong by 3.4 us. e7 has DVE behind both sums, later than that end had it: its gate product comes at 41.9, 2.8 us later than before the change, outside the bounds that I gave (gain 0.3 to 6.8). A further 1.4 us, with the features' 1.1 taken off, came behind the output product, which took 5.09 us in place of 6.62.

**Tables (11.5).** Right: from the gate product to the end of the scan's product 22.7 us became 11.2, 11.5 less. The Hankel table was issued at 17.5 and landed 9.0 us later, in the estimated 26 to 29 (so the third rival fails), the turning was done by 40.4, and ACT's eight copies ended at 44.8, just ahead of DVE's 45.4. All of it was covered, the last copies by 0.6 us.

**Norm ahead.** The mechanism is right. The forecast's 5.95 us from step to dense products was 5.8, the features cost 1.1, and e5 prices the net of steps 1 to 3 at 3.1, 3.9 and 3.4.

**Rounds behind q and the clock.** The step "copy to q at 10.7" left out that POOL's moved products stretch DVE's votes and x2 by 5.1 us, so that the chain to the gate product was 2.1 us longer than forecast. The clock cost 3.1 and 2.7 us at the output products of steps 2 and 3, where I took 1.0 out of a range of 0 to 2.9. But the up products behind gave 1.7 and 3.0 back, which the sum had not seen: net 1.4 lost in step 2 and 0.3 won in step 3, so 1.1 in all against 2.0 forecast. Step 3 came within 0.5 us of its forecast by this.

**POOL behind x1n (1.8 a step).** L1074 fell to 1.14 us as forecast. That the queue behind it "has over 20 us" was the wrong question: PE could wait, but DVE's query products lost 8 of the 12.9 us of POOL's lead and with it their free run, 2.1 us a step by e13. On the other side POOL's old order would have put two sums and 16 products beside DVE's head, where the new one puts 16 products; with both effects e13 prices the order at 3.9 and 5.3 us in steps 2 and 3.

**Query products (1.8 in step 1, 0, 0, 3.0).** By e6 the form alone is worth 0.5, 3.1, 3.2 and 3.4 in the new order: the total is larger, and it stands elsewhere. In steps 2 and 3 "shared work covers it" was wrong, since DVE was last over the slices. In step 1 the gain was also lost by a detail of the diff that I read and didn't cost: `QPART` 3 puts all 15 parts ahead of the last h, while before four of 29 stood behind it. e2 gives this back. The fourth rival (slow paired access patterns) did not come true. The second (a full exchange of turns with POOL) did not as told, but its mechanism was there, and one sign of being wrong came with it: a query product of 2.33 us on DVE in step 3, where 1.5 was the limit I had set.

**Sum of parts.** Each part undone alone costs step 2 3.9 (norm), 3.1 (query products) and 3.9 (POOL's order), 10.9 in all, where the whole change gave 4.4. Terms of a schedule with two engines in turn as last don't add.

## What to carry to other kernels

When work is moved off one engine's wait, list what then stands beside it on the others, and cost the neighbour as if it paid. Ask of each interleaved sequence what stands behind the last item of the chain; the cut of 15 parts gave 6.0 to 9.5 us over three steps, the norm's move 9.3 over four. Put leftover work only into a wait longer than itself, and read that wait's length in the profile first.

## What the runs showed of the hardware

A DVE instruction beside POOL can last as long as a whole train of POOL's, not one: 4.98 us for 0.33 (e13), 2.76 for 0.43. The Trainium skill says in "SBUF — State Buffer", section "Who interferes with whom", that DVE with two SBUF inputs, or in a mode that takes both ports, and POOL lock each other out for a whole instruction. The traces agree with a lock, and show several of POOL's instructions passing first. The 4.98 us fell on an instruction with one input; whether it used both ports no run here shows.

The clock behind a pause is not fixed by the kernel. After pauses of 3.2 to 3.5 us the same 16 records took 7.13, 8.61 or 10.19 us, and after the same work in step 1 the fall came either under the fillers or behind them, which is 1.9 us of the step. Two traces of the changed kernel agreed within 0.1 us on all marks; the two of the cut stand 8.7 us apart at the experts. Fillers have to be counted for the full clock: five took 4.56 us at it and 6.26 where it fell under them, and left a pause of 2.7 or 1.0 us.
